# Closing experts: late rows turned at later steps, late places in five pieces, their copies on ScalarE, last loads on two queues

## The reference

```python
h = jnp.mod(x_flat[:, :TOP_K].sum(axis=1).astype(jnp.int32), E)
sel = jnp.stack([h, jnp.mod(h + 1, E)], axis=1)
...
w = jnp.any(sel == e, axis=1).astype(x.dtype) / TOP_K
y = jnp.maximum(x_flat @ W1e + b1e, 0.0) @ W2e + b2e
return (acc + w[:, None] * y, None)
```

## Time and profile before

| | |
|---|---|
| median of three runs | 1483.82 us (1479.96 to 1485.55) |
| profiled execution | 1478.26 us, its span 1476.4 us |
| TensorE busy | 86% of the span |
| VectorE, ScalarE, GpSimd busy | 83%, 70%, 45% |
| closing | about 1370.6 us to the end, 105.8 us |

### The profile page before, as it was taken

The page is one execution under the profiler, slowest core; times in us unless marked ns, Lnnn a source line. Parts: engine busy times, 40 slices in busy tenths (PEclk is TensorE's granted clock), DMA queues, the critical chain, the costliest instruction groups (busy, mean ns, idle before and its releaser), DMA issues.

```text
span 1476.4 us, 22824 instructions
## 1 busy us (share of the span) xinstructions
PE 1263.8 (86%) x8424; PEld 498.1 (34%) x8424; DVE 1231.4 (83%) x1574; ACT 1034.7 (70%) x1832; POOL 662.6 (45%) x762
## 2 busy tenths in 40 slices
PE   4645789888977996887479999999999999999996
PEld 2211334333443443333212222222222222223896
DVE  3999988898989874666689999999999999982764
ACT  5541488678836833643249998999989998998654
POOL 1989878977978864624303001200020003430374
PEclk8767889999988998999669999999999999999999
DMA  8222132212322212430222115100010000002023
GB/s 238 83 77 86 57 95 79 85 60 86 93 71 86 88 29 67 101 90 22 45 65 52 31 31 84 23 3 2 2 24 2 2 2 2 20 28 56 19 76 117
DMA packets 83577, 84.15 MB, mean 57 GB/s; under 512 B 15497, under 2 KB 59018, under 8 KB 83466
## 3 DMA queue, kind: packets, MB, share of 16 engines
q1 hardware_dynamic: 80852, 77.47, 19.5%
q0 software_dynamic: 2496, 5.13, 1.0%
q10 hardware_dynamic: 118, 0.10, 0.0%
HBM read 66.45 MB, written 16.23 MB: 56 GB/s over the span
## 4 chain that ended last, share of the span: by engine, by line
PE 49%; DVE 25%; ACT 9%; issue 8%; POOL 7%; DMA 2%; DVEq 0%; ACTq 0%; POOLq 0%; SPq 0%
DVE mx L1836 14%; PE PS L1122 13%; PE PS L1110 7%; PE PS L858 5%; PE PS L1074 5%; PE PS L867 5%; PE PS L810 2%; POOL D L2060 2%; PE PS L1192 2%; DVE D L1613 2%; PE PS L1207 2%; ACT D L1321 1%; DVE PS L1592 1%; ACT L1321 1%; PE PS L776 1%
## 5 line engine op out<-in xcount | busy, mean ns | idle before, releaser
L1474 ACT ACTIVATE aa<-PS 128x512 f32<-128x512 f32 x1024 | 551.8, 598 | 51.2 <-PE PS L1110 41.0
L1836 DVE TENSOR_REDUCE mx<-PS 128x2 f32<-128x1024 f32 x480 | 551.8, 1216 | 10.2 <-PE PS L1074 8.1
L1122 PE MATMUL PS<-aa,D 128*32 128x256 f32 x4096 | 321.9, 392 | 1.5 <-ACT aa L1474 0.6
L1110 PE MATMUL PS<-D 54*128 54x512 bf16 x1024 | 215.8, 390 | 9.4 <-ACT aa L1474 9.4
L1074 PE MATMUL PS<-D 51*128 51x512 bf16 x960 | 194.2, 387 | 15.6 <-DVE mx L1836 13.0
L2168 POOL CAST n<-nm 16x128 bf16<-16x128 f32 x15 | 4.2, 282 | 409.3 <-ACT nm L1456 409.3
L867 PE MATMUL PS<-xnT,f_w 128*128 128x512 f32 x288 | 159.2, 647 | 7.7 <-ACT HB L1348 6.9
L1592 DVE TENSOR_TENSOR_SCAN PS<-PS,D 128x512 f32<-128x512 f32 x128 | 157.5, 1231 | 7.6
L1348 ACT ACTIVATE HB<-PS 128x512 f32<-128x512 f32 x144 | 84.0, 595 | 106.3 <-PE PS L867 99.2
L858 PE MATMUL PS<-HB,f_w 128*128 128x512 f32 x288 | 147.1, 620 | 6.8 <-DVE GO L1687 5.9
L1122 PEld LDWEIGHTS PS<-aa,D 128*32 128x32 f32 x4096 | 84.3, 108 | 195.3 <-issue 153.4
(11 more groups left out here) (385 smaller groups left out, 1667.1 us busy)
## 6 DMA issues: line engine op xcount, KB each, us to landing
D<-bc SPq DMA_DIRECT2D x128, 256.0 KB, 3.5
GB<-gd SPq DMA_DIRECT2D x32, 256.0 KB, 4.1
D<-sq SPq DMA_DIRECT2D x8, 384.0 KB, 5.6
xs<-zero SPq DMA_DIRECT2D x1, 2944.0 KB, 18.6
f_w<-in_L_ffn_experts_w SPq DMA_DIRECT2D x1, 2048.0 KB, 9.6
f_w<-in_L_ffn_experts_w SPq DMA_DIRECT2D x8, 256.0 KB, 6.1
aa<-in_L_ffn_W SPq DMA_DIRECT2D x8, 256.0 KB, 3.3
D<-in_L_ffn_W SPq DMA_DIRECT2D x8, 256.0 KB, 3.5
```

The source lines that it names most:

```text
L1110: e.matmul(take_exp(s + hh), KS[64 * hh:64 * hh + 54, p, 128 * kb:128 * kb + 128], QP[64 * hh:64 * hh + 54, qc % 2, p, :], start=True, sto ...
L1122: t = e.matmul(PS[32 * j:32 * j + 32, 7, cs], va[:, kb, 9 * h:9 * h + 32], Pt[K % 3][:, 512 * j + 256 * n:512 * j + 256 * n + 256], start= ...
L1474: e.activation(Pt[K % 3][:, c:c + 512], bank((s + hh) % 3), ACT.Exp).then_inc(S("e_free"), 1)
L1836: e.tensor_reduce(mx4[:, G % 2, :, pair, b, c:c + 1], max_banks(m), AX.X, ALU.max).then_inc(freed(m)[0], 1)
```

## The change

`sort_places` becomes a generator with four stops; the late call plays one of its five pieces at each of steps 10 to 14. The scatters and the load of the late rows go from step 12 to step 14. The turnings go from steps 22, 23, 24, 25 to 28, 32, 36, 40. ScalarE gets the copies of turned rows out of PSUM, and VectorE copies all late destinations at once at step 28. VectorE normalizes the late rows once, and ScalarE copies them into the second buffer at its own step 5. The last two loads are issued by SyncE and ScalarE, one each. The semaphore counts follow.

```diff
@@ -338,14 +338,14 @@
             p["choose"](3)
         elif u == 9:
             p["late_ranks"](maxs.take())
-        elif u == 10:
-            p["late_places"]()
-        elif u == 12:
-            for i in range(2 * LATE_TOKENS):
-                p["late_scatter"](i)
-            p["late_stage"]()
-        elif 22 <= u < 26:
-            p["late_column"](u - 22, maxs.take())
+        elif 10 <= u < 15:
+            p["late_places"](u - 10)
+            if u == 14:
+                for i in range(2 * LATE_TOKENS):
+                    p["late_scatter"](i)
+                p["late_stage"]()
+        elif u in (28, 32, 36, 40):
+            p["late_column"](u // 4 - 7, maxs.take())
         elif u == SORTED + LAG_SORTED + 1:
             p["gather"]()
         elif u in (39, 41, 43):
@@ -669,6 +669,11 @@
                 e.dma_start(KS[64 * hh + 48:64 * hh + 51, :, a:b],
                             sc[0:48, a:b].rearrange("(k a b) t -> b k a t", k=3, b=2)[hh]).then_inc(S(f"d_key{c}"), 16)
 
+        def rows_of(q, r):
+
+            a = 128 * SORTED_TOKENS * r + 512 * q if q < 3 else 2 * 128 * SORTED_TOKENS + 128 * LATE_TOKENS * r
+            return ys[a:a + 512, :].rearrange("(b p) d -> p b d", p=128)
+
         def down_sorted(u):
 
             return bank((4, 6, 7)[u % 3])[:, 0:128]
@@ -685,10 +690,12 @@
             e.tensor_scalar(odd, held, 12582912.0, None, ALU.add).then_inc(done, 1)
             w.wait_ge(done, n + 4)
             e.tensor_scalar(held, odd, 12582912.0, None, ALU.subtract).then_inc(done, 1)
+            yield
             for i, (step, src, dst) in enumerate(((1, held, odd), (2, odd, even), (4, even, incl))):
                 w.wait_ge(done, n + 5 + 2 * i)
                 e.tensor_copy(dst[:, 0:step], src[:, 0:step]).then_inc(done, 1)
                 e.tensor_tensor(dst[:, step:8], src[:, step:8], src[:, 0:8 - step], ALU.add).then_inc(done, 1)
+            yield
             w.wait_ge(done, n + 11)
             e.tensor_tensor(base, incl, held, ALU.subtract).then_inc(done, 1)
             w.wait_ge(done, n + 12)
@@ -1186,7 +1195,7 @@
             def sorted_up(u, s):
 
                 to = take_exp(s)
-                w.wait_ge(S("columns"), 16 if u < SORTED else 18 + 2 * ((u - SORTED) // 4))
+                w.wait_ge(S("columns"), 16 if u < SORTED else 18 + (u - SORTED) // 4)
                 w.wait_ge(S("own"), 2 * u + 2)
                 for j in range(4):
                     t = e.matmul(to[:, 128 * j:128 * j + 128], own[u % RING][:, 128 * j:128 * j + 128], columns(u),
@@ -1482,6 +1491,23 @@
                 e.activation(early_sort["RK"].rearrange("p b x -> p (b x)"), max_banks(m)[:, 0, 0:8 * SORTED_TOKENS + 8],
                              ACT.Copy).then_inc(freed(m)[0], 1)
 
+            def late_norm():
+                w.wait_ge(S("h_xn"), 12 + LATE_TOKENS)
+                e.activation(xn3[1][:, :, 0:128], xn3[0][:, :, 0:128], ACT.Copy).then_inc(S("h_xn"), 1)
+
+            def late_column(i, m):
+                n = min(4, LATE - 4 * i)
+                w.wait_ge(S("m_full"), m + 1)
+                w.wait_ge(S("columns"), 17)
+                e.activation(columns(SORTED + 4 * i, n), max_banks(m)[:, 0, 0:128 * n], ACT.Copy).then_inc(
+                    S("columns"), 1)
+                w.wait_ge(S("columns"), 18 + i)
+                e.sem_inc(freed(m)[0], 1)
+
+            def total():
+                w.wait_ge(S("d_ys3"), 16 * LATE)
+                e.dma_start(YC[:, 1, :, :], rows_of(3, 1)).then_inc(S("d_ya"), 16)
+
             def sorted_up(u, s):
                 w.wait_ge(S("e_full"), s + 1)
                 if u >= 5:
@@ -1494,7 +1520,8 @@
 
             slot = {}
             attention_order(ATT_IDLE | dict(finish=finish, score=score, evac=evac, turn=turn, heads=heads, ranks=ranks,
-                                            sorted_up=sorted_up))
+                                            late_norm=late_norm, late_column=late_column, sorted_up=sorted_up,
+                                            total=total))
 
         def vector_program(e):
             w = Waits(e)
@@ -1888,10 +1915,9 @@
                 w.wait_ge(S("h_st"), 32)
                 w.wait_ge(S("d_blank"), W_BLANK)
                 w.wait_ge(S("h_xn"), 12)
-                for r in range(2):
-                    for b in range(LATE_TOKENS):
-                        e.tensor_scalar(xn3[r][:, b, 0:128], x_tok[:, 12 + b, :], mv[:, 12 + b, 0:1],
-                                        rstd[:, 12 + b:13 + b], ALU.subtract, ALU.mult).then_inc(S("h_xn"), 1)
+                for b in range(LATE_TOKENS):
+                    e.tensor_scalar(xn3[0][:, b, 0:128], x_tok[:, 12 + b, :], mv[:, 12 + b, 0:1],
+                                    rstd[:, 12 + b:13 + b], ALU.subtract, ALU.mult).then_inc(S("h_xn"), 1)
 
             def choose(q):
 
@@ -1928,9 +1954,11 @@
                               max_banks(m)[:, 0, 0:8 * LATE_TOKENS + 8]).then_inc(freed(m)[0], 1)
                 w.wait_ge(*freed(m))
 
-            def late_places():
+            late_sorting = sort_places(e, w, S("late_place"), 6, late_sort, LATE_TOKENS, LATE, SORTED)
+
+            def late_places(i):
                 w.wait_ge(S("tabled"), SORT_TABLES)
-                sort_places(e, w, S("late_place"), 6, late_sort, LATE_TOKENS, LATE, SORTED)
+                pull(late_sorting)
 
             def column(i, m):
                 n = min(4, SORTED - 4 * i)
@@ -1942,14 +1970,9 @@
                 e.sem_inc(freed(m)[0], 1)
 
             def late_column(i, m):
-                n = min(4, LATE - 4 * i)
-                w.wait_ge(S("d_stage0"), 16 * 5)
-                e.tensor_copy(idsI[:, SORTED + 4 * i:SORTED + 4 * i + n], staged3[:, 4 * i:4 * i + n, 128]).then_inc(
-                    S("columns"), 1)
-                w.wait_ge(S("m_full"), m + 1)
-                e.tensor_copy(columns(SORTED + 4 * i, n), max_banks(m)[:, 0, 0:128 * n]).then_inc(S("columns"), 1)
-                w.wait_ge(S("columns"), 18 + 2 * i)
-                e.sem_inc(freed(m)[0], 1)
+                if i == 0:
+                    w.wait_ge(S("d_stage0"), 16 * 5)
+                    e.tensor_copy(idsI[:, SORTED:UNITS], staged3[:, :, 128]).then_inc(S("columns"), 1)
 
             def pick(u):
 
@@ -2272,7 +2295,7 @@
                 w.wait_ge(*freed(slot["rank"]))
                 w.wait_ge(S("tabled"), SORT_TABLES)
                 w.wait_ge(S("one_hot"), 3)
-                sort_places(e, w, S("place"), 42, early_sort, SORTED_TOKENS, SORTED, 0)
+                drain(sort_places(e, w, S("place"), 42, early_sort, SORTED_TOKENS, SORTED, 0))
 
             def scatter(r, b):
                 w.wait_ge(S("place"), 42 + PLACED)
@@ -2293,14 +2316,14 @@
             def late_scatter(i):
                 r, b = divmod(i, LATE_TOKENS)
                 w.wait_ge(S("late_place"), 6 + PLACED)
-                w.wait_ge(S("h_xn"), 12 + 2 * LATE_TOKENS)
+                w.wait_ge(S("h_xn"), 12 + LATE_TOKENS + 1)
                 w.wait_ge(S("d_xs"), 32 * SORTED_TOKENS)
                 e.indirect_dma_start(xs, bass.IndirectOffsetOnAxis(late_sort["placeI"][:, r, b:b + 1], 0), xn3[r][:, b, :],
                                      None).then_inc(S("d_xs"), 16)
 
             def sorted_out(u):
                 w.wait_ge(S("x_out"), u + 1)
-                w.wait_ge(S("columns"), 16 if u < SORTED else 18 + 2 * ((u - SORTED) // 4))
+                w.wait_ge(S("columns"), 16 if u < SORTED else 17)
                 e.indirect_dma_start(ys, bass.IndirectOffsetOnAxis(idsI[:, u:u + 1], 0), Ys[u], None).then_inc(
                     S("d_ys" if u < SORTED else "d_ys3"), 16)
 
@@ -2500,10 +2523,6 @@
                 e.dma_start(staged3, xs[128 * SORTED:128 * UNITS, :].rearrange("(b p) d -> p b d", p=128)).then_inc(
                     S("d_stage0"), 16)
 
-            def rows_of(q, r):
-                a = 128 * SORTED_TOKENS * r + 512 * q if q < 3 else 2 * 128 * SORTED_TOKENS + 128 * LATE_TOKENS * r
-                return ys[a:a + 512, :].rearrange("(b p) d -> p b d", p=128)
-
             def gather():
                 w.wait_ge(S("d_ys"), 16 * SORTED)
                 for q in range(3):
@@ -2516,8 +2535,7 @@
 
             def total():
                 w.wait_ge(S("d_ys3"), 16 * LATE)
-                for r in range(2):
-                    e.dma_start(YC[:, r, :, :], rows_of(3, r)).then_inc(S("d_ya"), 16)
+                e.dma_start(YC[:, 0, :, :], rows_of(3, 0)).then_inc(S("d_ya"), 16)
                 w.wait_ge(S("added"), 8)
                 e.dma_start(ov[:, 12:16, :], x_tok[:, 12:16, :]).then_inc(S("d_out"), 16)
 
```

## The result

| | before | after |
|---|---|---|
| median | 1482.53 us (1479.96 to 1486.18, 6 runs) | 1472.15 us (1471.61 to 1476.26, 6 runs) |
| profiled execution, its span | 1478.26, 1476.4 | 1471.61, 1469.9 |
| closing (first up product to the end) | 105.8 | 99.1 |
| of it up to the start of TensorE's last matmul | 94.0 | 87.0 |

The ratio is 0.9931, with a 95% interval of 0.9912 to 0.995. Two later comparisons, on two chips, give 0.9954 (0.9934 to 0.9974) and 0.9948 (0.9933 to 0.9964). The changed kernel is about 0.5% faster, with 0.7% in the first comparison. The forecast was 1476.4 in a range from 1472.5 to 1481.0: the median lies 4.25 us under the one and 0.35 us outside the other.

What follows compares the result with a forecast made beforehand. TensorE sets the closing's pace, with two holes. 2.5 (places) + 5.3 (late rows, clock) - 0.95 (copy) + 0.3 (one-hot) + 0.3 (loads) = 7.45 us, so 1483.8 - 7.45 = 1476.4, range 1472.5 to 1481.

Steps and rivals of the forecast that it cites:

- Places: Sorting of places on VectorE, in five pieces: TensorE's hole before unit 11's down product goes, 2.5 us gained.
- Late rows: Turnings at steps 28, 32, 36, 40: TensorE's load wait 3.4, low clock 1.7 and 0.2 go, 5.3 us.
- Evacuations on ScalarE: Four copies of turned rows, 0.6 us each, fit into ScalarE's steps with a turning: no cost.
- The copy: ScalarE's step 5 waits for VectorE's normalizations, so unit 5's down product is 0.95 us late (0.7 to 1.3).
- One-hot: VectorE is 1.1 us early, so the ranks no longer wait for the one-hot: 0.3 us back.
- Last loads: Final two loads on two queues: 0.3 us gained, between 0.8 and nothing if they only slow each other.
- GpSimd and the gather: Unit 30's output leaves GpSimd at 1434.3; VectorE waits 0.7 us for gathered rows at step 39, 1.26 free.
- A: Rival for the whole kernel: the sum as above, gain 6.3 to 8.2 us, 1475.6 to 1477.5; chance 0.66.
- B: Rival: GpSimd's gather comes late, TensorE stalls at unit 40, 3.0 us of gain go, 1479.4; chance 0.14.
- C: Rival: ScalarE's step 5 costs more, 2.2 us or more in all, 1477.6 to 1478.5; chance 0.06.
- E: Rival: the hole at unit 5 lowers TensorE's clock, a step 1.6 us more, possibly over 1491; chance 0.04.
- D: Rival: the copy is hidden or two queues give 0.8; gain 8.3 or more, 1475.5 or less; chance 0.10.

Runs made afterwards that it cites:

- pieces_turn22: The changed kernel with the late rows turned at steps 22 to 25 again: 1481.04 us, ratio 1.0009 to the kernel before.
- norm_vector: The changed kernel with VectorE doing all eight normalizations again and no copy on ScalarE: ratio 0.9953, closing 100.1 us.
- after_again: The changed kernel, unchanged, measured again: 1472.15 us, ratio 0.9954 to the kernel before.
- turn_late_only: The kernel before with only the late rows' turnings moved to steps 28, 32, 36, 40: 1476.97 us, ratio 0.997.
- copy7_adds_again: The changed kernel with ScalarE's copy at step 7, adds at steps 41, 43, 45, both last loads on SyncE: 1474.35 us, ratio 0.9954.
- base_third: The kernel before, unchanged, measured again: 1477.80 us, ratio 0.9991.
- base_fourth: The kernel before, unchanged, measured again: 1481.12 us, ratio 1.0011.

## Why the forecast came out as it did

**The base was the step that failed.** The forecast's sum against the profiled execution was 1470.8, and that execution took 1471.61: 0.8 us off. The miss came in the next sentence, "The median of the runs shown is 5.6 us above it, and the gain is the same: 1483.8 - 7.45 = 1476.4". Three runs had caught the kernel before at the upper end of its times: on three chips without the gaps 115 runs have a median of 1479.58. The profiled execution (1478.26, clock 0.926) was nearer to what most runs do than the median of three was, and the difference has nothing to do with the closing. The range allowed for it, by 0.35 us too little. The 6.4 us of the closings, taken from 1478.26, give 1471.9. Chance played on the other side as well: five of the six runs of the changed kernel had a clock of 0.926 or more. At 0.921 to 0.925 it takes 1476.2 (three runs), next to the forecast's 1476.4, and a median there would have been a hit by luck.

**The five terms** against the profiled pair, forecast gain 7.45, closing 6.7:
- Places, 2.5: right. The hole is gone and all three profiles of the changed kernel have TensorE full from unit 5's down product on, and the last one starts at 1456.99 (forecast near 1456.6). pieces_turn22 shows it is no gain without the next.
- Late rows, 3.4 + 1.7 + 0.2: right in the profiled pair. The load went out at 1410.61 and landed after 6.3 us, near 1416.9 (forecast 1416.6), 5 us ahead of the turning. That the 1.7 belongs to the late rows was wrong as a rule: in three of five profiles with the first hole the clock fell behind that.
- Evacuations on ScalarE, no cost: right. No wait of TensorE stands behind the turnings.
- The copy, -0.95: 1.13 by unit 8 (0.84 plus the 0.3 of the next term), 0.2 more; the PE part is 7.0 shorter where the forecast has 7.15. Within its 0.7 to 1.3.
- One-hot, +0.3: right; norm_vector brings the wait back, and its down product of unit 8 is again 19.42 after the first up product, as before.
- Last loads, +0.3: wrong in sign, -0.3. This is the whole of the rest. "If they only slow each other, nothing" was no lower end: they can slow each other by more than the issue saves. The Trainium skill (DMA: Bandwidth & Descriptors, Issuing engines are not separate DMA queues) gives two queues a gain, if a small one, the time of the initiation; the runs show a loss of 0.3 instead, and they decide.

**GpSimd and the gather:** as forecast in the profiled execution. Unit 30's output left at 1434.87 (forecast 1434.3), VectorE waited 0.4 us (0.7). The free 1.26 us can be read off five profiles without gaps: waits of 0.4 and 0.6 leave the tail at 12.1 and 12.0, one of 1.7 gives 12.5 (1.7 - 1.26 = 0.44), with one queue 1.5 gives 12.0 against the 11.8 without wait (0.24), and 2.6 gives 13.7 (1.34 of 1.6). That the wait differs by 1.3 us between profiles of the same kernel was not in the forecast: the gather went out 66.3 us after the first up product in two and 67.3 in after_again. TensorE never stalled behind it, as none was over 3.5. turn_late_only, with 0.9, has a tail 0.3 above before, which this does not explain. So the slack is read across profiles and not shown by an edit: the runs meant to test it fell on the chips with the pauses, and copy7_adds_again moved three things at once.

**The rivals.** A is what happened in the profiled pair, at its lower end (6.3 to 8.2, got 6.65). B, the late gather, did not come in full; GpSimd kept its pace, 27 starts in the 35.55 us from the first scatter to unit 30's output, 1.32 each. C and E did not come: the copy took 0.63, and the clock stayed at 1.00 behind the hole of 0.9. My argument against E leant on the hole of 2.3 us that left the clock at 1.00; base_third and base_fourth show that such a hole can lower it. D's 8.3 or more is what the medians showed and no closing did. "Within 0.5% or faster" stays as near to a draw as forecast: 0.9931, 0.9954 and 0.9948 stand on both sides of the bound.

## What to carry to other kernels

Before a gain is taken off a median of few runs, see where the kernel's runs lie: compare the profiled execution's granted clock and the start of the changed stage with other executions, and compare stages, which repeat to 1 us here where the whole varies by 10. Two holes on one engine in a row are one edit: the first closed alone makes the second longer (5.0 for 3.4), and a price that hangs on "some hole" is paid until the last is closed. When the engine that sets the pace gets faster, count the side queue that it overtakes in free microseconds, and move its consumer by as many steps.

## What was not expected of the hardware

- The kernel before has one fall of the granted clock per closing, from 1.00 to about 0.65 over 5 us, in one pair of profiles behind a hole of 3.4 and 3.5 us and in the other pair behind one of 2.5 us some 20 us earlier, with the same instructions. In the first pair a hole of 2.3 and 2.5 us there left it at 1.00, in the other pair the later hole of 2.8 and 2.6 did.
- Two loads issued at the same time from SyncE and ScalarE landed after 3.5 and 4.1 us; from SyncE alone, 0.4 apart, they landed after 3.0 and 3.4. The slower one was always ScalarE's (4.0 to 4.1 in four profiles).
- On two of the chips the issue of TensorE, ScalarE and VectorE had pauses of 0.3 to 2 us over some 10 us at one place, without a releaser, and a lower clock behind it; the same program ran without them on another chip.
